# An audio tower on one core: W_o split once under the folding for all five tiles, and the second group's scales moved between two gate products

## The reference

```python
h = patches @ W_tok.T + b
x = layernorm(h)
q, k, v = x @ Wq.T, x @ Wk.T, x @ Wv.T
q, k = rope(q), rope(k)
s = causal(q @ k.T / sqrt(32))
heavy = argmax_over_keys(sum_over_queries(softmax(s)))
p = softmax(where(heavy | band, s, min))
h = h + (p @ v) @ Wo.T
g, u = split(layernorm(h) @ w_gate_up.T)
out = h + (silu(g) * u) @ w_down.T
```

## Time and profile before

| | us |
|---|---|
| median of 3 runs | 268.24 |
| lowest, highest | 267.89, 269.38 |
| the profiled execution | 268.19 |
| its span in the trace | 266.4 |
| PE busy | 257.1 |
| DVE busy | 169.9 |
| ACT busy | 108.2 |
| POOL busy | 48.9 |

### The profile page before, as it was taken

The page is one execution under the profiler, slowest core; times in us unless marked ns, Lnnn a source line. Parts: engine busy times, 40 slices in busy tenths (PEclk is TensorE's granted clock), DMA queues, the critical chain, the costliest instruction groups (busy, mean ns, idle before and its releaser), DMA issues.

```text
span 266.4 us, 5045 instructions
## 1 busy us (share of the span) xinstructions
PE 257.1 (96%) x1909; PEld 213.5 (80%) x1909; DVE 169.9 (64%) x333; ACT 108.2 (41%) x181; POOL 48.9 (18%) x53
## 2 busy tenths in 40 slices
PE   7999999799999999989999999999999999999993
PEld 5466498575887887867888879999999999999992
DVE  1696998997899987899976775633333333343323
ACT  2311212863285454749531053533443333344320
POOL 0116032004001121100100101422222222222210
PEclk9999999999999999999999999999999999999999
DMA  6996003005359999983890050694333344400004
GB/s 220 416 418 220 1 4 122 2 2 100 59 161 232 290 252 288 271 270 135 219 285 12 0 198 5 168 336 127 119 118 118 118 121 126 128 19 0 0 0 118
DMA packets 13154, 38.61 MB, mean 145 GB/s; under 512 B 1864, under 2 KB 1936, under 8 KB 12496
## 3 DMA queue, kind: packets, MB, share of 16 engines
q1 hardware_dynamic: 11120, 32.17, 35.2%
q0 software_dynamic: 1728, 5.81, 11.5%
q10 hardware_dynamic: 288, 0.39, 0.4%
HBM read 31.24 MB, written 1.31 MB: 122 GB/s over the span
## 4 chain that ended last, share of the span: by engine, by line
PE 78%; DMA 8%; DVE 6%; ACT 3%; issue 3%; SPq 1%; POOL 0%; DVEq 0%; POOLq 0%
PE ps L225 49%; PE ps L1345 5%; PE ps L1223 5%; PE ps L1118 4%; DMA wgu<-stage 3%; PE ps L1326 3%; DMA stage<-w_ffn 3%; PE ps L1238 3%; PE ps L1185 3%; PE ps L1144 2%; DMA dims<-w_dims 2%; PE ps L1127 1%; PE ps L1069 1%; PE ps L1155 1%; DVE xT L724 1%
## 5 line engine op out<-in xcount | busy, mean ns | idle before, releaser
L225 PE MATMUL ps<-xT,wgu 128*128 128x384 f32 x384 | 70.5, 339 | 0.2 <-DVE gu L931 0.2
L225 PEld LDWEIGHTS ps<-xT,wgu 128*128 128x128 f32 x384 | 68.1, 188 | 1.8 <-issue 0.6
L931 DVE TENSOR_TENSOR gu<-silu,ps 128x256 f32<-128x256 f32 (+1 forms) x32 | 15.5, 485 | 47.5 <-PE ps L225 44.4
L363 POOL TENSOR_TENSOR wd<-stage,wd 128x512 fp32r<-128x512 f32 x16 | 26.2, 1636 | 77.1 <-ACT wd L431 77.1
L225 PE MATMUL ps<-wd,hT 128*128 128x512 f32 x156 | 38.8, 393 | 0.0
L591 ACT ACTIVATE silu<-ps 128x256 f32<-128x256 f32 (+1 forms) x32 | 14.0, 437 | 52.7 <-PE ps L225 52.2
L225 PEld LDWEIGHTS ps<-wd,hT 128*128 128x128 f32 x156 | 29.0, 188 | 5.4
L225 PE MATMUL ps<-xs,wgu 128*128 128x256 f32 x240 | 31.9, 289 | 0.9 <-DMA wgu<-stage 0.9
L225 PEld LDWEIGHTS ps<-xs,wgu 128*128 128x128 f32 x240 | 28.8, 188 | 4.6 <-issue 4.1
L431 ACT ACTIVATE wgu<-stage 128x1024 fp32r<-128x1024 f32 x20 | 21.1, 1056 | 24.4 <-PE ps L225 23.1
L1345 PE MATMUL ps<-stage,gu 128*128 128x512 f32 x56 | 26.3, 593 | 0.0
(11 more groups left out here) (126 smaller groups left out, 318.3 us busy)
## 6 DMA issues: line engine op xcount, KB each, us to landing
stage<-w_ffn SPq DMA_DIRECT2D x32, 512.0 KB, 4.5
stage<-w_ffn SPq DMA_DIRECT2D x32, 256.0 KB, 4.0
wgu<-stage POOLq DMA_DIRECT2D x6, 512.0 KB, 8.3
wd<-stage POOLq DMA_DIRECT2D x3, 512.0 KB, 7.0
stage<-w_k SPq DMA_DIRECT2D x1, 1024.0 KB, 6.6
stage<-w_q SPq DMA_DIRECT2D x1, 1024.0 KB, 10.1
stage<-w_v SPq DMA_DIRECT2D x1, 1024.0 KB, 12.1
wo<-w_o SPq DMA_DIRECT2D x1, 1024.0 KB, 15.2
```

The lines of the kernel that those rows point to most:

```text
L225: ins = pe.matmul(dst, lhs[a], rhs[b], start=first and n == 0, stop=last and n == 2)
L363: pool.tensor_tensor(dst, src, f32(hi), ALU.subtract).then_inc(done, 1)
L931: dve.tensor_tensor(gu[:, ring, cols], silu[:, ring, cols], ps[:, up, at:at + P * TILES[p]], ALU.mult)\
```

## The change

- W_o is loaded into slot 3 of `stage`; the tile `wo` is gone. ACT makes both copies right after the fold of W_q's bias (`minus_wo` between `folded_bias(1)` and `folded(2)`), POOL issues the sum behind the first spread of biases. Block 3's first load, which stood behind W_o's, now waits for that sum.
- All five tiles are projected with split operands, so units 0 and 1 get a low part too (`low_attn(0)`, `low_attn(1)` on DVE). `project_out` does the products in the order high-high, high-low, low-high and waits for the low part of the attention only before the last four.
- DVE: the maximum, clamp and subtraction of the second masked softmax of group 0 stand behind the first four value products; the statistics, scales and norms of the first pass are in another order. ACT: `exponential(3)` stands behind six drains, `hi_attn(0)` ahead of the table load for silu.
- PE: `project_biases("v", 1)` goes ahead of block 0's gate product for tile 1, and the scales of group 1 (`spread_scale(1)`) between those of blocks 0 and 1.
- SP: blocks 6 and 7 are loaded ahead of 4 and 5; in the middle blocks the down loads are three blocks late instead of one, so no gate and up load waits behind a down product there.
- Block 13's down product is split like those of 14 and 15 (`SD = 13`). The split of block 15's down weights moves behind its silu on DVE. In block 14, ACT copies the second pass's first weights (`hi_gu(0, 0, 0)`) before it waits for the block's product.
- Buffers are laid over each other in another way.

```diff
+SD = 13
+ND = NB - SD
...
-            sp.dma_start(wo[:, :, :].rearrange("p k n -> p (k n)"), w_o).then_inc(dma_wo, 16)
+            sp.dma_start(stage[:, 3, :], w_o).then_inc(dma_wo, 16)
...
-            gate_up_load(3)
-            down_load(3)
-            for x in range(3):
+            for x in range(2):
                 sp.wait_ge(fold_bias_mm, x + 1)
                 gate_up_load(x)
                 down_load(x)
-
+            sp.wait_ge(fold_bias_mm, 3)
+            gate_up_load(2)
+            down_load(2)
+            sp.wait_ge(wo_high, 1)
+            sp.wait_ge(dma_wo_low, 16)
+            gate_up_load(3)
+            down_load(3)
+
+            next_gate_up(2)
+            next_gate_up(3)
             next_gate_up(0)
-            for i in range(1, NB):
+            next_gate_up(1)
+            next_down(0)
+            for i in range(4, S2 + 1):
+                next_gate_up(i)
+                next_down(i - 3)
...
@@ gpsimd
             spread_bias(0)
+            low_wo()
             key_add(2)
...
                 low_weights(i)
-            low_wo()
@@ scalar
             folded_bias(1)
+            minus_wo()
             folded(2)
...
             exponential(2)
-            exponential(3)
             for item in DRAIN[3:9]:
                 drain(item)
+            exponential(3)
+            hi_attn(0)
             act.wait_ge(neghalf_set, 1)
             act.activation(warm[:, :], neghalf[:, :], ACT.Silu)
             minus_weights(2)
-            hi_attn(0)
...
-            minus_wo()
             first_pass(11)
-            hi_wo()
...
-            first_pass(14)
+            silu_gate(A, 14, 0)
             hi_gu(0, 0, 0)
+            hi_units(14)
             hi_xT(LN2[2])
             hi_xT(LN2[4])
             hi_xT(LN2[3])
+            hi_weights_down(15)
             first_pass(15)
@@ vector
             softmax_in(2)
-            softmax_in(3)
+            mask(SOFTMAX[3][2])
             softmax_out(2)
             values(0, 7, 6, 5, 4)
+            softmax_in(3, unmasked=False)
+            statistics(3)
             softmax_out(3)
+            low_attn(0)
             values(0, 3, 2, 1, 0)
-            statistics(3)
             statistics(4)
+            statistics(LN2[1])
+            low_attn(1)
+            normalise(LN2[1])
             token_scale(3)
+            statistics(LN2[0])
             token_scale(4)
-            statistics(LN2[1])
-            normalise(LN2[1])
-            statistics(LN2[0])
             normalise(LN2[0])
             tables(1)
@@ tensor
             def project_out(t, units, last):
-                pe.wait_ge(dma_wo, 16)
                 pe.wait_ge(attn_sb, units)
+                pe.wait_ge(wo_high, 1)
+                pe.wait_ge(dma_wo_low, 16)
                 read_out(*last)
...
+                for a, b in ((0, 0), (0, 1), (1, 0)):
+                    if a:
+                        pe.wait_ge(attn_lo, units)
+                    for k in range(KT):
+                        ins = pe.matmul(ps[:, WO_BANK[t], :], xT[:, a, k, P * t:P * (t + 1)], wo_parts[:, b, k],
+                                        start=a + b + k == 0, stop=a == 1 and k == KT - 1)
...
             transposes(LN2[1], ("wo", 1))
+            project_biases("v", 1)
+            pe.wait_ge(xf_sb, 1)
+            gate_up_whole(0, 1)
             read_out("projection", ("q", 1, 1))
             pe.wait_ge(apart_set, NT)
             spread_scale(1)
-            pe.wait_ge(xf_sb, 1)
-            gate_up_whole(0, 1)
             gate_up_whole(1, 1)
             transposes(LN2[0], ("wo", 0))
-            project_biases("v", 1)
```

119 lines of the change are left out of this document (60 added, 59 removed).

## The result

The changed kernel takes 267.7 us (median; 266.58 to 268.35) against 268.34 us of the kernel before in the same comparison: a ratio of 0.9954, 95% interval 0.9931 to 0.9976. It is faster, by 0.2 to 0.7%. Set against the 268.24 from which the forecast started, this ratio makes 267.0 us: inside the range of 264.9 to 267.4, but above the 266.4 up to which the forecast's own case reached. The forecast of 265.9 is a ratio of 0.9913, outside the interval. The sign was right, and the expected gain about twice the one that came. By the prediction's own border between faster and same, 0.5% or 266.9, this is still the case "same", by a hair; that the interval leaves out 1 is owed to the thirteen executions of each kernel.

What follows compares the result with a forecast made beforehand. PE, busy 96% of the span, was taken to bound the kernel, so only less work or closed gaps help. Gains of 0.7 + 1.1 + 0.5 = 2.3 off 268.19 gave 265.9 us, range 264.9 to 267.4.

Steps and rivals of the forecast that it cites:

- the forecast's own case: Whole kernel: all three gains come, 265.9 us, running from 264.9 to 266.4 by its own bounds; chance 0.52.
- Part 1: Front of group 0's values: earlier value products and split projections gain 0.7 us, bounds 0.2 and 1.3.
- The wait of 1 us inside tile 0's projection: Front: PE has its eight products ready about 1 us early and waits for DVE's low part, a new wait.
- the scales' own products: Front, ahead of block 1's product: two small scale products on PE, costed at 0.2 us.
- Part 2: Loads in the middle blocks: block 10's wait for its sum, costing 1.12, closes; gain 1.1 us, bounds 0.5 and 1.1.
- block 4's load would be late: Rival, first pass: load queued behind blocks 6 and 7, copy 4.1 late, PE waits 2.7, 269.2 us; chance 0.07.
- One sign: Middle blocks, in the changed kernel's trace: landings of block 4 to 10's sums under 8.5 us.
- closed is closed: Block 10's gap: reason for the upper bound of 1.1 us, the same as the expected gain.
- it doesn't do what it says: Rival, middle: another sum becomes last or DVE's block 11 product holds PE; half given back, 266.5 us; chance 0.1.
- Part 3: End of the first pass: shorter down product and no gap entering the second pass; gain 0.5 us, bounds 0.2 and 0.7.
- The split product: Block 13's down product: six split products of 1.52 us replace four whole ones of 1.88, 0.35 less on PE.
- The gap: Entry of the second pass: PE's 0.21 us wait for DVE goes, since ACT and DVE come 0.9 earlier.

Runs made afterwards that it cites:

- e1: The changed kernel with 32 bytes of padding ahead of xs, against the kernel before: ratio 0.9933.
- e4: The changed kernel with block 3's loads ahead of block 2's, against the kernel before: ratio 0.9962.
- e9: The changed kernel with 192 bytes of padding ahead of xs and block 3's loads ahead of block 2's, against the kernel before: ratio 0.9925.
- e12: e9 with block 11's product on DVE between the two value products ahead of it, against the kernel before: 266.68 us, ratio 0.9905.
- e8: The kernel before with only ACT's copy of the second pass's first weights moved ahead of its wait for block 14's product: ratio 0.9991.
- e6: The changed kernel with 64 bytes of padding ahead of wgu, moving wgu, wd and xs together, against the kernel before: ratio 0.9953.
- e5: The changed kernel with 64 bytes of padding ahead of xs, against the kernel before: ratio 0.9932.
- e3: The changed kernel with the kernel before's order of SP loads, against the kernel before: ratio 0.9992.
- e10: The changed kernel with 128 bytes of padding ahead of xs, measured in one execution: 267.27 us.

## Why the prediction was half right

**Part 1, forecast 0.7, came 0.5.** The chain was right to 0.2 us, read from the head: the first low part began at 58.29 - 0.56 = 57.7 (forecast 57.9), tile 1's gate product at 67.08 - 0.56 = 66.5 (66.6), the scales at 68.6 (68.7). The wait of 1 us inside tile 0's projection was half of that (0.5 in e1, e4, e9, e12), and hidden behind the fetch stall in the changed kernel's own trace, whose gap ahead of the value sums went from 1.43 to nothing for the same reason. The term that was mis-sized is the scales' own products, costed at 0.2: they take 0.44 to the next start. The prediction had both transposes' cover at 1.29 and did not see that in the order before a small piece of work stood under each, and now under one.

**Part 2, forecast 1.1, came 1.1 in this pair of traces, and less in general.** The mechanism holds: less traffic from 77 to 97, the landing's median down from 8.2 to 5.3, no wait. That block 4's load would be late didn't happen: its copy waited 0.76 until 78.26, before 0.63 until 78.10. One sign was missed narrowly: a sum took 8.6 where the prediction had all under 8.5, but it was block 6's and nobody waited for it. Two things were missed. The forecast took the gap of one execution as the kernel's own, while two of five executions with the old order don't have it; and "closed is closed" was wrong at full pace, where DVE's product of block 11 gives 0.3 back. The rival "it doesn't do what it says" had named that product; in the changed kernel the slower pace hides it.

**Part 3, forecast 0.5, came 0.6, and 0.9 at the pace of before (e9, e12).** The split product gave 0.24 instead of 0.35: the forecast took the difference of two busy times, 1.88 and half of 3.04, though both run past the next start; from start to start it is 1.72 and 1.48. The gap gave 0.38 instead of 0.21, since a wait costs more than the idle time in its row. The upper bound had said so. The rest, some 0.3 in the projections and the products around them, the forecast had at nothing, and no run takes it apart.

**The step that failed.** "Buffers are laid over each other in another way" stands in the change, and no term of the sum does. It was put at nothing without a reason, and it cost 12 x 0.12 = 1.4 us, more than half of the forecast's 2.3, by the pace of the 288 gate and up products between 76 and 133 us, and 0.2 more in the last two blocks. With the pace of before restored, e9 gives 0.9925 and e12 0.9905; the forecast's 0.9913 lies in both intervals. Both kernels also have block 3's loads first, and e12 another order on DVE. So the sum was about right for the kernel that was reasoned about, and wrong for the kernel as laid out. That the measured time lies inside the range is luck: the range was closed at 267.4 for a small wait, and the loss was not a wait. No rival covered it: the one called "it doesn't do what it says" looked for the loss in waits, and this one is in the duration of instructions.

## What to carry to other kernels

When a change lays buffers anew, compare the mean duration of every group of matmuls before and after: a pace that is 3% off shows in no wait, no idle time and no instruction order. When an order is changed, ask of each small piece of work what it was covering and what it stands under now. Padding that mends one pair of operands moves others, so compare them all again. And look at a gap that a DMA makes in more than one execution before it goes into a sum.

## What was not expected of the hardware

The start of a moving operand against that of the weights sets the pace of split products: the same 24 matmuls take 3.31 us at one distance and 3.44 at another, and 32 bytes of padding change it (table above). At distance 0 the weight loads are longer too, 192 ns in the median against 188:

```profile
L227 PEld LDWEIGHTS ps<-xs,wgu x240: 187/192/192, 82.3 to 157.7; 128*128 128x128 f32 x120
```

```profile
L225 PEld LDWEIGHTS ps<-xs,wgu x240: 186/188/192, 82.1 to 157.7; 128*128 128x128 f32 x120
```

At 32 (e1) they are 188 again while the products are still slow, so the weight loads are not all of it. The Trainium skill (SBUF — State Buffer, "SBUF: two separate sides") says that PE never waits on another engine for its ports. Nothing here speaks against it: what moved are PE's two operands against each other. In e8, at the distance of the kernel before, two blocks at the start took 4.55 nevertheless, and in e9 one took 4.54; that stays open.

A queue of kind "instruction" shares the DMA engines with the data, and PE stands still when its packets are late. With four loads issued within 1.3 us and the engines busy 0.96, the packet came 3.5 us later than before, and PE stood 1.64 us (1.68 in e6, 1.14 in e5, 0.65 in e1, 0.59 in e3, none in e10 and none in e4, e9 and e12 with the loads spread). In one of the two executions with a stall of 1.6 to 1.7 us the granted clock then fell to 0.50 for some 3 us, and PE came 1.5 us later to tile 0's gate product; in the other it stayed at 1.00.
